# Transformer block with a mixture of experts: first rows modulated and turned earlier in the setup, and the router's product as one fp32 product

## The reference

```python
x = x + xcond(layernorm(x), cond, ctx)      # adaLN block: self attention, cross attention, gated FF
x = x + moe(layernorm(x), wqkv, w1, w2)

def adaln(x, t, w, b):                      # w: 128 x 256
    scale, shift = split(t @ w + b)
    return layernorm(x) * (1 + scale) + shift
def mha(xq, ctx, wq, wk, wv, wo, bo):       # 16 heads of 64; softmax(q k^T / 8) v, then wo
def glu_ff(x, w1, b1, w2, b2):              # (a * gelu(gate)) @ w2 + b2, hidden 512
def moe(x, wqkv, w1, w2):                   # 8 experts, top 2
    q, k, v = split(x @ wqkv.T)             # wqkv: 24 x 128, the router's product
    attn = softmax(q[:, :, None] * k[:, None, :]); logits = attn @ v
    # top 2 of 8 logits, softmax over the two, then silu(x w1a) * (x w1g) @ w2 of these experts
```

## Time and profile before

| | |
|---|---|
| time, median of 3 runs (lowest, highest) | 2151.15 us (2149.22, 2152.4) |
| profiled execution, its own time | 2138.83 us |
| its span | 2137.1 us |
| busy: PE, PEld | 2049.8 (96%), 1347.9 (63%) |
| busy: ACT, DVE, POOL | 1392.3 (65%), 1334.3 (62%), 1067.5 (50%) |
| granted TensorE clock, mean | 0.987 |

### The profile page before, as it was taken

One profiled execution on the slowest core, in us unless ns is written; L12 is line 12 of the kernel. 1 busy time (PEld: TensorE's weight loads), 2 busy tenths in 40 slices (PEclk: granted clock), 3 DMA queues, 4 the chain that ended last, 5 costly groups with the idle time before them and its releaser, 6 DMA issues. The chain is left out here.

```text
span 2137.1 us, 38900 instructions
## 1 busy us (share of the span) xinstructions
PE 2049.8 (96%) x11132; PEld 1347.9 (63%) x11132; DVE 1334.3 (62%) x3405; ACT 1392.3 (65%) x2665; POOL 1067.5 (50%) x1198
## 2 busy tenths in 40 slices
PE   6899999999999999999999999999999888899996
PEld 5455565655556555555555555656565548799996
DVE  4564657676767676767676766666656645466565
ACT  4566666666666666667676767676766656666663
POOL 1443444546464636363636373737372535465654
PEclk9999999999999999999999999999999999999998
DMA  4101111111111111112111111111112312122257
GB/s 133 45 29 41 50 35 50 46 50 45 49 44 49 44 49 44 49 44 54 44 49 44 49 44 49 44 49 44 52 47 69 98 44 59 40 67 66 73 180 217
DMA packets 136322, 127.36 MB, mean 60 GB/s; under 512 B 14665, under 2 KB 110569, under 8 KB 136234
## 3 DMA queue, kind: packets, MB, share of 16 engines
q1 hardware_dynamic: 127466, 109.11, 18.3%
q0 software_dynamic: 8768, 17.20, 2.4%
HBM read 86.63 MB, written 40.67 MB: 60 GB/s over the span
## 5 line engine op out<-in xcount | busy, mean ns | idle before, releaser
L1866 POOL TENSOR_TENSOR pr<-pr,sm 128x512 f32<-128x512 f32 x256 | 277.5, 1097 | 492.4 <-DVE sm L1419 492.4
L1095 ACT ACTIVATE kp<-ps 128x512 f32<-128x512 f32 x512 | 298.3, 600 | 182.1 <-PE ps L281 180.3
L816 PE MATMUL ps<-tt,V 128*128 128x512 f32 x768 | 381.8, 595 | 3.5 <-ACT tt L1095 3.5
L1409 DVE TENSOR_REDUCE mx<-ps 128x8 f32<-128x512 f32 x256 | 176.7, 690 | 313.3 <-PE ps L765 313.3
L1095 ACT ACTIVATE tt<-ps 128x512 f32<-128x512 f32 x512 | 274.9, 590 | 40.3 <-PE ps L795 40.3
L765 PE MATMUL ps<-kp,hf 128*64 128x256 f32 x2048 | 277.8, 393 | 7.2 <-DVE pr L1412 3.8
L281 PE MATMUL ps<-cT,M 128*128 128x512 f32 x768 | 261.8, 464 | 0.0
L765 PEld LDWEIGHTS ps<-kp,hf 128*64 128x64 f32 x2048 | 124.7, 136 | 197.3 <-DVE pr L1412 135.4
L1095 ACT ACTIVATE pt<-ps 128x512 f32<-128x512 f32 x256 | 153.5, 600 | 142.7 <-PE ps L777 142.7
L281 PE MATMUL ps<-hk,M 128*128 128x512 f32 x768 | 243.7, 440 | 1.9 <-DVE hk L1473 1.9
L922 PE MATMUL ps<-xT,wt 128*128 128x128 f32 (+1 forms) x1728 | 222.7, 279 | 5.7 <-ACT sl L1268 2.9
(11 more groups left out here) (228 smaller groups left out, 3498.1 us busy)
## 6 DMA issues: line engine op xcount, KB each, us to landing
mod<-emb_s SPq DMA_DIRECT2D x96, 256.0 KB, 4.3
xr<-rows_s SPq DMA_DIRECT2D x144, 66.0 KB, 1.9
cb<-y_s SPq DMA_DIRECT2D x32, 256.0 KB, 5.2
x_in<-in_x_dram SPq DMA_DIRECT2D x16, 256.0 KB, 4.4
xn_s<-x_in SPq DMA_DIRECT2D x16, 256.0 KB, 2.0
res<-xn_s SPq DMA_DIRECT2D x16, 256.0 KB, 2.8
c_in<-in_ctx_dram SPq DMA_DIRECT2D x16, 256.0 KB, 4.8
y_s<-res SPq DMA_DIRECT2D x16, 256.0 KB, 2.1
```

The source lines that it names most:

```text
L816: mm = nc.tensor.matmul(psO[:], Vw[a][:, g * HG + head_at(h), :], tt[:, h, :], start=(g == 0 and h == 0), stop=ends)
L1095: return nc.scalar.activation(o, i, ACT.Copy)
L1409: nc.vector.tensor_reduce(mx[:, p % 2, :], heads(psS[p % 2][:]), AX_X, ALU.max).then_inc(max_done, 1)
L1866: tensor(v, v, sm[:, p, :].unsqueeze(2).broadcast_to([P, HG, 64]), ALU.mult).then_inc(prob_done, 1)
```

## The change

It has three parts.

1. The order of the start. The first chunk's normalised rows are made on VectorE ahead of the first "T" copies (`ln1_norm`), and the modulated rows ahead of the "M" copies (`ln1_mod`). TensorE turns them after the "M" products and ahead of the "V" products (NV = N1 - 4 = 12), and into psO (bank ps7), which nothing else uses in the setup (`ln_bank`). ScalarE copies them ahead of its "V" copies, VectorE makes the low part ahead of its own.
2. The first keys wait for VectorE's copies only as far as "M" (NV); a key whose bank is psH (ps3), which the last "V" product used, waits for all of them (N1). This is the third key. The "E" products of norms 2 and 3, with their copies, move behind the second attention's products.
3. The router's product. ScalarE copies the turned rows whole, in fp32, into `hr`; VectorE's subtraction goes (16 times 128 x 512), and TensorE makes 4 plain fp32 matmuls of 24 columns in place of 12 fp32r ones. WR is kept once, in fp32, and copied by ScalarE (16 columns) and VectorE (8). `hr` lies in the memory of tb2, a table on one partition that is built at other times. The bank's release for later stages is ScalarE's copy (hx_hi[3]), and the wait of `ln_hi` for the router ahead of writing h3 goes.

```diff
-        tb2 = sb("tb2", [1, 2, TMX, E])
+        tb_hr = sb("tb_hr", [P, 2 * TMX * E])
+        tb2 = tb_hr[0:1].rearrange("p (k n e) -> p k n e", k=2, e=E)
+        hr = tb_hr[:, 0:CT]
-            WR = sa("WR", [P, 2, 3 * E], F32R)
+            WR = sa("WR", [P, 3 * E])
...
-        tiles += [("E", 1), ("E", 2)] + attention_tiles(1) + [("R",)]
+        NV = N1 - H // 4
+        tiles += attention_tiles(1) + [("E", 1), ("E", 2), ("R",)]
+        def ln_bank(c, k):
+            return psO if first(c) and k == 0 else psM
-                  ((2, 2, "back2", y2_done), (4, 3, "ln4", hx_lo[3]), (7, 3, "router", mix_cp)),
+                  ((2, 2, "back2", y2_done), (4, 3, "ln4", hx_hi[3]), (7, 3, "router", mix_cp)),
... # TensorE
-                    mm = mm3(psM[:, t * 3 * E:(t + 1) * 3 * E], lambda k: h3[:, k, t * P:(t + 1) * P], lambda k: WR[:, k, :])
+                    mm = nc.tensor.matmul(psM[:, t * 3 * E:(t + 1) * 3 * E], hr[:, t * P:(t + 1) * P], WR[:], start=True, stop=True)
-            setup(0, N1)
-            pe.wait_ge(su_dve, N1)
+            setup(0, NV)
             pe.wait_ge(mods[0], 2)
-            turn4(psM, hx[0], lambda t: h1[:, t, :])
+            turn4(ln_bank(0, 0), hx[0], lambda t: h1[:, t, :])
+            setup(NV, N1)
+            pe.wait_ge(su_dve, NV)
             for h in range(HG):
+                if key_bank(0, h) is psH:
+                    pe.wait_ge(su_dve, N1)
                 keys(0, 0, h)
... # ScalarE
-                    op = copy(WR[:, 0, :], ps[:, 0:3 * E])
+                    op = copy(WR[:, 0:2 * E], ps[:, 0:2 * E])
             def ln_hi(c, k):
                 act.wait_ge(hx[k], c + 1)
-                if k == 2 and not first(c):
-                    act.wait_ge(rm_done, c)
-                if k < 2:
-                    copy(hf[k][:], psM[:]).then_inc(hx_hi[k], 1)
-                if k != 1:
-                    copy((hk if k == 0 else h3)[:, 0, :], psM[:]).then_inc(hx_hi[k], 1)
+                if k != 2:
+                    copy(hr if k == 3 else hf[k][:], ln_bank(c, k)[:]).then_inc(hx_hi[k], 1)
+                if k in (0, 2):
+                    copy((hk if k == 0 else h3)[:, 0, :], ln_bank(c, k)[:]).then_inc(hx_hi[k], 1)
-            setup(0, N1)
+            setup(0, NV)
             ln_hi(0, 0)
+            setup(NV, N1)
... # VectorE
-                    op = tensor(WR[:, 1, :], ps[:, 0:3 * E], f32(WR[:, 0, :]), ALU.subtract)
+                    op = nc.vector.tensor_copy(WR[:, 2 * E:], ps[:, 2 * E:3 * E])
-                         1: ((3, 2, after_attn2), (4, 2, stats3), (5, 3, lambda c: ln_lo(c, 3)), (6, 2, norm3), (8, -1, ln1_stats)),
+                         1: ((3, 2, after_attn2), (4, 2, stats3), (6, 2, norm3), (8, -1, ln1_stats)),
             setup(0, NE)
             ln1_stats(0)
-            setup(NE, N1 - H // 4)
-            ln1(0)
-            setup(N1 - H // 4, N1)
+            ln1_norm(0)
+            setup(NE, NV - H // 4)
+            ln1_mod(0)
+            setup(NV - H // 4, NV)
             ln_lo(0, 0)
+            setup(NV, N1)
             setup(N1, NSU)
```

More of the change, by code:

```diff
@@ L122, in pixart_block_moe @@
         TMX = TB * BODIES[0]
-        tb2 = sb("tb2", [1, 2, TMX, E])
+        tb_hr = sb("tb_hr", [P, 2 * TMX * E])
+        tb2 = tb_hr[0:1].rearrange("p (k n e) -> p k n e", k=2, e=E)
+        hr = tb_hr[:, 0:CT]
         tb3 = sb("tb3", [1, 4, TMX])
         n1 = CT * (GROUPS[0][1] - GROUPS[0][0]) // P
-        tb1 = tb2[0:1, 0].rearrange("p a e -> p (a e)")[:, 0:E * n1].rearrange("p (e n) -> p e n", e=E)
+        tb1 = tb_hr[0:1, 0:E * n1].rearrange("p (e n) -> p e n", e=E)
         with ExitStack() as phase_a:
@@ L244, in pixart_block_moe @@
         hx_hi = [sem(f"hx_hi{k}") for k in range(4)]
-        hx_lo = [sem("hx_lo0"), None, sem("hx_lo2"), sem("hx_lo3")]
+        hx_lo = [sem("hx_lo0"), None, sem("hx_lo2")]
         tm_done = sem("tm_done")
@@ L1455, in ln1, with ln1_norm, ln1_mod @@
             def ln1(c):
+                ln1_norm(c)
+                ln1_mod(c)
+            def ln1_norm(c):
                 dve.wait_ge(rstd[0], 5 * c + 5)
                 ln_norm(0, x_in, x_in)
+            def ln1_mod(c):
                 dve.wait_ge(nrm[0], c + 1)
@@ L1472, in ln_lo @@
                 dst = hk if k == 0 else h3
-                tensor(dst[:, 1, :], psM[:], f32(dst[:, 0, :]), ALU.subtract).then_inc(hx_lo[k], 1)
+                tensor(dst[:, 1, :], ln_bank(c, k)[:], f32(dst[:, 0, :]), ALU.subtract).then_inc(hx_lo[k], 1)
             tiles3 = lambda ap: ap.rearrange("p (t d) -> p t d", t=NT)
```

## The result

| | before | changed |
|---|---|---|
| time, median of 4 runs each | 2150.68 us (2149.22 to 2152.4) | 2137.51 us (2134.62 to 2140.15) |
| profiled execution, own time | 2138.83 us | 2140.15 us |
| its span | 2137.1 us | 2138.4 us |
| busy PE, DVE | 2049.8, 1334.3 | 2045.5, 1321.4 |

The ratio is 0.9938, 95% interval 0.9921 to 0.9955: 13.2 us faster, and 1.0 us above the 2136.5 that were forecast. The two profiled executions alone say the opposite, 1.3 us slower; experiment 4 shows why they must not be subtracted.

A forecast was written before the change was run, and what follows sets the result against it. TensorE was taken to bound the rounds, and waits plus a low clock the start. Start 7.7 us and router 7.0 us, 14.7 in all, taken from 2151.15, gave 2136.5 us; range 2129 to 2144.

The forecast's parts named there:

- The wait for `mod`: Start, VectorE: modulated rows must wait for the loads of `mod`, landing at 18.8 us, a new wait of 0.9 us.
- the turn waits for nothing: Start, TensorE: modulated rows are done at 20.6 us, when the M products have just finished, so no wait.
- Keys: Start, TensorE: the first key matmuls start at about 23.9 us in place of 29.62, a gain of 5.7 us.
- Clock: Start, TensorE: without the long hole the keys run at full clock, saving 1.66 us (7.40 to 5.74), bounds 0 to 1.66.
- the start gives about half: Rival, 14%: `mod` lands later or the clock falls again; start gains 4 us, 11 in all, time 2140 us.
- The start in sum: Setup up to VectorE's first reduction: 5.7 + 1.66 + 0.35 = 7.7 us earlier.
- `place`: Two narrow fp32 matmuls of 32 columns, 0.093 us a record, taken as price for the router's product: 0.74 to 0.83 us.
- The price of the R product: Router's product, slow bound: at the R product's 0.24 us a record, eight take 1.92 us, losing 10.7 us in all.
- the serial load: Rival, 2%: router's weight load and product run in a row, 2.75 us for 1.25; 24 us lost, time 2167.
- the double price: Rival, 4%: an fp32 record costs twice an fp32r one, router's product 1.66 us, time 2150, no change.
- The router in sum: Rounds, TensorE: 0.46 us saved per product, sixteen products, the last two counted half: 7.0 us.
- only the start counts: Rival, 12%: the router's part saves nothing (0.156 us a record, or something behind the product is last); time 2143.5 us.

The follow-up runs named there:

- experiment 4: The kernel before, unchanged, profiled a second time: one run 2149.09 us beside a median of 2150.74; profiled span 2147.3 us.
- experiment 6: Changed kernel with each router product made twice into the same columns: 2136.74 us against 2138.53 for the kernel before, ratio 0.9991.
- experiment 5: Changed kernel with VectorE's router subtraction and the bank's wait for it put back, result unused: 2127.0 us against 2138.53 for the kernel before, ratio 0.995.
- experiment 3: New start alone, router as before, with the E products back between first keys and second attention's T products: 2144.91 us against 2150.74 before, ratio 0.9973.
- experiment 8: Changed kernel with the W1 and W2 copies and splits right behind the second attention's T copies: 2128.0 us against 2138.53 before, ratio 0.9946.
- experiment 9: Changed kernel, unchanged, profiled and timed once more: 2141.47 us against 2151.14 for the kernel before, ratio 0.9957.
- experiment 2: Changed kernel with the router's part taken back, so the new start alone: 2142.32 us against 2150.74 for the kernel before, ratio 0.9965.
- experiment 10: Changed kernel with VectorE making the modulated rows behind the four M subtractions: 2145.96 us against 2151.14 for the kernel before, ratio 0.9978.
- experiment 12: Changed kernel with reordered loads, earlier W splits, an E product between T and M, normalised rows behind the third T copy: 2122.3 us against 2137.78 before, ratio 0.9929.
- experiment 11: Changed kernel with reordered loads, W splits behind the second attention's T copies, an E product between T and M: 2140.28 us against 2151.14 before, ratio 0.995.

## Why the prediction was right

The time, 2137.5, lies 1.0 us above the forecast. The mechanism came as told, but both of its terms were too large, and that the time met the forecast so closely is in part luck. By its steps:

- **The bound.** Right. In the rounds TensorE sets the pace: 0.89 us put on it per round came out as 0.83 to 0.87 (experiment 6 against the changed kernel's two profiles, 104.90 and 104.86), and 0.68 us on VectorE as nothing (experiment 5).
- **The wait for `mod`.** The mechanism was right, its size was mis-sized: I put the landing at 18.8, and it came at 19.50 (18.43 to 19.48 in experiments 3, 5, 6, 8 and 9, where VectorE waited for it too). The loads went out at 13.8, as before (13.7); 3.8 to 4.3 us to landing was too little, the same view of the changed kernel has 3.9 to 4.8. VectorE idled 1.90 us instead of 0.9, and the step "the turn waits for nothing" failed: it waited 0.89.
- **Keys.** Forecast 23.9, was 24.90. 0.7 of this is the landing. The other 0.3 is a step that named the wrong last comer: I let the keys wait for the low part of hk (23.8) and the fourth V product for its bank. The low part was done at 24.36, half a microsecond early; what is last is TensorE's own row of V products, 2.88 us behind the turn's 0.60. From landing to keys it takes 5.40 us in the changed kernel and in experiments 3 and 9 alike, where I had 5.1. That the M products started at 17.75, near the old 18.03, was luck: they start 1 us later where the clock rises later (experiment 2), and I had no term for that.
- **Clock.** Right for the keys: 5.75 us instead of 7.40. That it falls later, under the first scores, I had not seen; it cost nothing there. Experiment 10 shows the other side of the rival "the start gives about half": had the rows been 3.5 us later, all of the gain at the first reduction would have gone.
- **E products.** 0.31 us by experiment 3, for 0.35.
- **The start in sum.** 7.0 us by the reduction against experiment 4 (52.35 to 45.39), 6.7 against the first profile, for 7.7; timed alone 7.5.
- **The router's product.** 0.81 us, 0.101 a record, inside the forecast's 0.74 to 0.83. `place` was the right row. The price of the R product (1.92 us), the serial load (2.75) and the double price (1.66) are all ruled out. The Trainium skill's four passes for true fp32 (FP8 and Floating Point Precision, TensorE Precision Notes), which I named against this part, don't set the price at 24 columns in this trace.
- **The router in sum.** This step failed in size. The step was "saves 0.46, sixteen times, half of the last two": 0.44 went from each product, but 0.30 to 0.35 from each round, 4.2 us over twelve in the changed kernel's first profile, and 0.35 to 0.4 were lost ahead of the first product. The loss of 0.1 us a round was taken as nothing. By the 13th product the changed kernel is ahead by 1597.59 - 1586.82 = 10.8 us against experiment 4, by the 16th by 1897.31 - 1887.96 = 9.4, and by the end by 8.9. What the last three products bring can't be read from one pair: the new start alone was ahead by 7.0 us at the 13th product and by 9.6 at the end. Timed alone the part gave 3.4 us for 7.0.
- **The base.** 12.3 us between profile and median were carried over unexplained. Experiment 4 shows why that did no harm: 10.2 of them lay behind the rounds, and the holes there come and go with the chip and not with the change. The prediction had no reason for it.
- **The sum.** 14.7 us were forecast. The spans give 8.9, the parts timed alone 10.9, experiment 5, which differs from the changed kernel by a subtraction worth nothing, 10.7, and the two timings of the whole 13.2 and 9.3 (0.9957 of 2150.7). So the mechanism brings some 4 us less than I worked out, most of it in the router's part, and that the first timing met the forecast within 1 us is in part its scatter. By the second, 2141.4 us, the rival "only the start counts" (2143.5) is nearer than the forecast; the router alone speaks against it, since its interval (1.5 to 5.4 us) leaves out zero, and so does a round that is 0.30 to 0.35 us shorter in every profile with this part (but for experiment 6, where the product is made twice).

## What to carry to other kernels

On a path where one engine waits for a chain of others, put the chain's first steps into that engine's and its neighbours' idle time before they are due, and read from the trace what is then late next: here a transfer whose landing moved by a microsecond between executions. Holes of over 3 us on TensorE cost twice here, once by themselves and once by the clock behind them, so a delay that opens one can take back the whole gain; and how late the clock first rises moves the start by a microsecond too. An instruction taken from the busy engine need not give the round its full time back, and a profile should be compared only with one whose untouched stages last equally long. Several kernels' profiles lined up at the same landmarks (first reduction, first and 13th product) show in which stretch a loss is made, and that it can lie where the edited instructions don't even run.

## What the runs showed that I had not expected

- One hole of 3.32 us on TensorE was followed by a clock of 0.50 for 10.2 us, most of it full work (experiment 10). One of 2.13 us among T products that were still slow went with a clock that rose only at 30.98 us, 15 us later than in experiment 12, which has no such hole. No fall followed the holes of 1.02 us ahead of the M products, yet in the changed kernel the clock fell at 42.89 with no longer hole than 0.74 us near it.
- From 0.22 us each, T products go to 0.12 when the clock first rises, and this moment differs by 3.5 us between executions (14.75 to 18.30, experiment 11 aside).
- Narrow fp32 matmuls cost 0.101 us a record, as narrow fp32r ones do, though wide ones cost 3.5 times as much as fp32r ones.
- The same program has a 0.75 us hole in every fourth expert tile on two of four chips, and the medians of before differ there by 12 to 13 us from those on the other two.
